# A three-way windowed attention kernel: the wide projection moved ahead of the third unit of scores

## The chip, the cores and the metric

The kernel runs on one core of one Trainium2 chip. The metric is the device time of one launch in microseconds (us). Engines go by short names: PE (TensorE, matmuls), ACT (ScalarE), DVE (VectorE), POOL (GpSimd), SP (SyncE, which here only issues transposing DMAs).

## What is computed

The input is 128 x 256 x 192. A tokenizer stage first turns each of the 128 sequences of 256 rows into 127 pooled rows of 192 (a gated softmax over windows of four). Then come an attention block and a feed-forward block, each on a layer norm of its input and each added back. The reference of the attention block, cut to what matters:

```python
qkv = (x @ w_qkv.T).reshape(B, N, 3, H, hd)        # H = 8 heads, hd = 24, thirds of 8
q3, q4, q5 = thirds(q); k3, k4, k5 = thirds(k); v3, v4, v5 = thirds(v)
x3 = attn(q4, cat(k3, k4), cat(v3, v4))            # softmax(q k^T * scale) v
x4 = attn(q5, cat(k3, k5), cat(v3, v5))
x5 = attn(q5, cat(k4, k5), cat(v4, v5))
out = cat(x3, x4, x5) @ w_proj.T + b_proj
h = h + out
```

## The kernel before

One block is one sequence (127 rows of 192), and there are NB = 128 blocks. The function `attend` runs the whole attention stage as a software pipeline written out by hand: every engine has a `body(i, r)`, called for i = -4 to 130 (r is i modulo 4), and in body i the engines work on different blocks. Engines meet only through semaphores, each engine takes its instructions in the order in which the body writes them, and all transposing DMAs go through SP in the order of its body.

In one body PE does, in this order:

- `products(i, r, 0)` to `products(i, r, 3)`, four *units* of two heads. A unit has six matmuls of *scores* (L583) into three PSUM tiles, `p_s1`, `p_s5` and `p_s0`, for block i, and four matmuls of *maxima* (L587) into `p_maxa` (two matmuls of 384 columns) and `p_maxb`. The maxima are plain q k^T products that serve only to find each row's largest value for a later block: block i+1 in units 0 and 1, block i+2 in units 2 and 3.
- between the units: `outputs` (L653, probabilities times values, into `p_o`; eight matmuls after unit 0, eight after unit 1, eight after unit 3), `qkv(i)` (the *wide projection* of block i+3 into `p_z`, five matmuls of 512 columns, L620 to L626, after unit 2), `outputs_t` (three transposes of `ot`, L664, after the wide projection) and `proj` (the output projection of block i-2, also into `p_z`, after unit 3).

ACT does three exponentials a unit, each of 128x512: of `p_s1` (L696), `p_s5` (L700) and `p_s0` (L703). After unit 1 it copies `p_o` to `ot` (L712), and after the exponentials of unit 2 it copies the wide projection out of `p_z`, the q and k part to `raw` (L721), the v part to `vn` (L722). There is one `p_z`, so `proj` waits for the copy to `vn`.

DVE reduces `p_maxa` (L746) and `p_maxb` (L750) in each unit, takes the layer norm's statistics (L757, `bn_stats`), writes the maxima into the operand `qk` (L766, L767), normalizes (L773, L776) and adds `proj` to the residual (L783). Each of the tiles `p_s1`, `p_s5`, `p_s0`, `p_maxa` and `p_maxb` exists once, so the matmuls of one unit wait for the readers of the unit before: `p_s0` for L703, `p_maxa` for L746, `p_maxb` for L750.

POOL splits `raw` into high and low halves in `qk` (`halves`, L801 to L812). SP then transposes: `kt` and `qt` (needed by the maxima of unit 2 in the next body), `qm` (needed by the scores), `xt` (needed by the wide projection) and `yt` (needed by `proj`).

Of the kernel before, what the change touches and what calls it, by code (L numbers as in the profile page):

```python
# [12 lines left out]
C = 192  # L13
# [437 lines left out]
def attend(nc, t, NB):  # L451

    with ExitStack() as ctx:
# [3 lines left out]
        U = 4  # L457
        NQ, NK = 3 * HEADS, 3 * HEADS
        K0 = NQ * 32
# [62 lines left out]
        def _(sp):  # L522
# [6 lines left out]
            def body(i, r):  # L529
# [5 lines left out]
                if within(i + 2, NB):  # L535
                    ready(pool_k, seen(i + 3))
                    if within(i - 2, NB):
                        ready(pe_s0[3], seen(i - 1))
                    sp.dma_start_transpose(kt[:, (r + 2) % U].rearrange("p k g n -> p (k g) n"), qk[:, r % 2, K0:K0 + 768]).then_inc(dma_k, 16)
                    ready(pool_q, seen(i + 3))  # L540
                    if within(i, NB):
                        ready(pe_ma[1], seen(2 * (i + 1)))
                        ready(pe_mb[1], seen(i + 1))
                    sp.dma_start_transpose(qt[:, r % 2].rearrange("p k g n -> p (k g) n"), qk[:, r % 2, 0:512]).then_inc(dma_q, 16)
# [24 lines left out]
        def _(pe):  # L569
# [3 lines left out]
            def products(i, r, u):  # L573
# [15 lines left out]

                if has_s:  # L590
# [4 lines left out]
                if has_m:  # L595
                    if u == 2:
                        pe.wait_ge(dma_k, seen(16 * (bm + 1)))
                        pe.wait_ge(dma_q, seen(16 * (bm + 1)))
                    pe.wait_ge(dve_ma[u - 1], seen(i + 2 if u < 3 else i + 3))
                    maximum(p_ma[:, 0:3, :], c, 1, slice(0, 3)).then_inc(pe_ma[u], 1)  # L600
                    maximum(p_ma[:, 4:7, :], d, 1, slice(0, 3)).then_inc(pe_ma[u], 1)
                if has_s:
                    score(p_s[1][:, 2:4, :], b, 1, slice(0, 3, 2)).then_inc(pe_s1[u], 1)
                if has_s:
                    pe.wait_ge(act_e5[u - 1] if u else act_e5[3], seen(i + 1 if u else i))
                    score(p_s5[:, 0:2, :], fifth, 2, slice(1, 3), 0)
                    score(p_s5[:, 2:4, :], fifth, 2, slice(1, 3), 1).then_inc(pe_half[u], 1)
# [20 lines left out]
            def qkv(i):  # L628
                if within(i + 3, NB):
                    pe.wait_ge(dma_x, seen(16 * (i + 4)))  # L630
                    pe.wait_ge(*z_reader(i, 0))
                    rows(p_z[:, :], xt, "wqkv").then_inc(pe_qkv, 1)
# [34 lines left out]
            def body(i, r):  # L667
# [10 lines left out]
                outputs(i - 1, before, 1, 2)  # L678

                products(i, r, 2)  # L680
                qkv(i)
# [9 lines left out]
        def _(act):  # L691
# [14 lines left out]
            def body(i, r):  # L706
# [7 lines left out]
                exponentials(i, r, 2)  # L714
# [9 lines left out]

                exponentials(i, r, 3)
# [484 lines left out]
```

## Time and profile before

| | |
|---|---|
| three runs | 1880.60, 1873.08, 1877.03 us; median 1877.03 us |
| the profiled execution | 1871.97 us, its span 1870.2 us |
| busy in the span | PE 94%, DVE 80%, ACT 77%, POOL 67%, PE's weight loads 54% |
| mean granted TensorE clock | 0.981 of full |
| attention stage | its first wide projection starts at 343.0 us, its last output projection at 1418.6 us |

A matmul's end is modelled, so a high busy share of PE is no proof that PE never waits: what a wait costs has to be read off the start times. Views that follow later are read like this. A row of a timeline is start (us), duration (us), engine, line, operation, output<-input tiles, shapes and count; square brackets hold the idle time of the engine just before it and who ended it, and rows between two "..." are left out. A row of the windows view holds the window's bounds, its length, busy us (and instructions) of PE, PE's weight loads, DVE, ACT and POOL, the granted TensorE clock as a share of full, the share of DMA time and GB/s. A grouped row holds line, engine, operation, tiles and count, then busy us and mean ns of one, then idle us of the engine just before them and who ended it. A DMA row ends with the median us from issue to landing.

The tokenizer comes before the attention stage and the feed-forward block after it; the change touches neither.

### The profile page before, as it was taken

The page shows a single profiled execution, that of the slowest core. Times are in us where ns is not written, and L with a number is a line of the kernel's source. Part 1 is how long each engine was busy: PE and PEld are TensorE (multiplying, and loading weights), DVE is VectorE, ACT ScalarE, POOL GpSimd, SP SyncE. Part 2 cuts the span into 40 slices and gives each one's busy share as a digit, 9 for nine tenths or more (in the row PEclk, how much of TensorE's full clock was granted, in tenths as well). Part 3 has the DMA queues.
Part 4 walks back from the last instruction along what each step waited for, and adds up shares of the span by engine and source line. Part 5 has one row for each costly group of instructions (what it writes and reads, how often), then busy time and mean ns, then how long its engine had stood idle before and what let it go on. Part 6 is the DMA issues. An engine that isn't in the chain of part 4 may idle for free. (4 is left out here: it accounts for less than half of the span.)

```text
span 1870.2 us, 56704 instructions
## 1 busy us (share of the span) xinstructions
PE 1749.2 (94%) x19008; PEld 1016.4 (54%) x19008; DVE 1498.9 (80%) x3546; ACT 1444.0 (77%) x2983; POOL 1251.8 (67%) x2306
## 2 busy tenths in 40 slices
PE   5999999589999999999999999999994999999999
PEld 3677777144444444444444444444442777777776
DVE  6877778589999999999999999999984555555554
ACT  4666666288888888888888888888884777777775
POOL 5777776477777777777777777777753565656661
PEclk9999999599999999999999999999997999999999
DMA  7344442154444444444444444444441333333332
GB/s 192 95 111 111 111 111 67 39 83 89 86 90 89 89 87 90 89 89 87 89 90 88 89 89 90 88 89 89 89 76 28 71 69 69 70 67 70 67 74 54
DMA packets 503935, 159.49 MB, mean 85 GB/s; under 512 B 452176, under 2 KB 503120, under 8 KB 503888
## 3 DMA queue, kind: packets, MB, share of 16 engines
q1 hardware_dynamic: 503888, 158.90, 40.1%
q8 instruction: 26, 0.43, 0.1%
q14 instruction: 21, 0.17, 0.0%
HBM read 37.26 MB, written 12.48 MB: 27 GB/s over the span
## 5 line engine op out<-in xcount | busy, mean ns | idle before, releaser
L746 DVE TENSOR_REDUCE tops<-p_maxa 128x6 f32<-128x762 f32 x512 | 483.7, 945 | 50.5 <-PE p_maxa L587 38.9
L653 PE MATMUL p_o<-probs,vn 127*32 127x256 f32 x6144 | 410.7, 385 | 0.4 <-DVE att L776 0.4
L696 ACT ACTIVATE probs<-p_s 128x512 f32<-128x512 f32 x512 | 306.3, 598 | 126.6 <-PE p_s L583 126.3
L583 PE MATMUL p_s<-qm,kt 32*128 32x256 f16 x3072 | 369.9, 272 | 3.3
L750 DVE TENSOR_REDUCE tops<-p_maxb 128x4 f32<-128x508 f32 x512 | 346.6, 677 | 0.0
L703 ACT ACTIVATE probs<-p_s 128x512 f32<-128x512 f32 x512 | 310.9, 607 | 0.0
L700 ACT ACTIVATE probs<-p_s 128x512 f32<-128x512 f32 x512 | 304.0, 594 | 0.0
L1055 DVE TENSOR_TENSOR gel_lo<-gel,gel_hi 128x512 f16<-128x512 f32 x192 | 151.2, 788 | 168.1 <-ACT gel_hi L1027 168.1
L583 PEld LDWEIGHTS p_s<-qm,kt 32*128 32x128 f16 x3072 | 149.3, 92 | 229.3 <-issue 126.4
L801 POOL TENSOR_TENSOR qk<-raw,one 128x384 f16<-128x384 f32 x128 | 105.7, 826 | 228.2 <-ACT raw L721 228.2
L653 PEld LDWEIGHTS p_o<-probs,vn 127*32 127x32 f32 x6144 | 160.5, 109 | 140.6 <-issue 74.4
L1019 ACT ACTIVATE gel<-f_w,b 128x512 f32<-128x512 f32 x192 | 131.9, 687 | 117.4 <-PE f_w L968 117.4
L587 PE MATMUL p_maxa<-kt,qt 24*128 24x384 f16 x1024 | 173.4, 333 | 37.3 <-issue 18.8
L587 PE MATMUL p_maxb<-kt,qt 24*128 24x256 f16 x1024 | 196.5, 272 | 0.2
L979 PE MATMUL f_y<-w_hi,gel_hi 128*128 128x192 f16 x768 | 188.8, 246 | 0.2 <-DVE gel_lo L1055 0.2
L981 PE MATMUL f_y<-w_hi,gel_lo 128*128 128x192 f16 x768 | 188.9, 246 | 0.0
L980 PE MATMUL f_y<-w_lo,gel_hi 128*128 128x192 f16 x768 | 188.8, 246 | 0.0
L1125 POOL TENSOR_TENSOR f_hx<-f_hn,f_one 128x192 f16<-128x192 f32 x120 | 85.5, 712 | 153.7 <-ACT f_hn L1006 151.0
L208 ACT ACTIVATE tanhs<-pa 128x384 f32<-128x384 f32 x128 | 62.7, 490 | 99.2 <-PE pa L154 99.2
L1027 ACT ACTIVATE gel_hi<-gel 128x512 f16<-128x512 f32 x192 | 120.9, 630 | 7.0
L396 POOL TENSOR_TENSOR diag<-ident,weight 128x256 f32<-128x256 f32 x128 | 79.2, 620 | 54.1 <-DVE weight L296 44.9
L183 PE MATMUL ph<-zs,band 128*128 128x192 f32 x512 | 105.4, 330 | 3.1 <-DVE band L317 2.2
(212 smaller groups left out, 4509.9 us busy)
## 6 DMA issues: line engine op xcount, KB each, us to landing
xt_a<-in_xt SPq DMA_DIRECT2D x32, 512.0 KB, 4.4
xt_b<-in_xt SPq DMA_DIRECT2D x64, 256.0 KB, 5.1
out<-out_sb SPq DMA_DIRECT2D x32, 336.0 KB, 2.6
xt<-hx SPq DMA_TRANSPOSE x128, 2.4
kt<-qk SPq DMA_TRANSPOSE x128, 2.8
qt<-qk SPq DMA_TRANSPOSE x128, 2.4
qm<-qk SPq DMA_TRANSPOSE x128, 2.7
yt<-ay SPq DMA_TRANSPOSE x128, 2.3
```

Source lines behind the costliest of these rows:

```text
L583: return nc.tensor.matmul(o, kt[full(j), r, kind, half, :], qm[full(j), r % 2, versions, half, :], start=True, stop=True, skip_group_check ...
L587: return nc.tensor.matmul(o, qt[short(j), rq, kind, half, :], kt[short(j), rk, cols, half, :], start=True, stop=True, skip_group_check=True)
L653: last = nc.tensor.matmul(p_o[32 * j:32 * j + 32, blocks, :], vn[0:NP, r, src:src + 32], probs[0:NP, r % 2, QUAD * g + j, kind * 256:(kind ...
L696: nc.scalar.activation(probs[:, r % 2, h + 1, 0:512], p_s[1][:, :, :].rearrange("p x n -> p (x n)"), ACT.Exp, scale=SCALE).then_inc(act_e1 ...
L700: nc.scalar.activation(probs[:, r % 2, fifth:HEADS:QUAD, 512:768], p_s5[:, :, :].rearrange("p (h x) n -> p h (x n)", h=2), ACT.Exp, scale= ...
L703: nc.scalar.activation(probs[:, r % 2, h, 0:512], p_s[0][:, :, :].rearrange("p x n -> p (x n)"), ACT.Exp, scale=SCALE).then_inc(act_e0[u], 1)
L746: nc.vector.tensor_reduce(top[:, q, 6 * pair:6 * pair + 6].rearrange("p (e k) -> p e k", e=2), p_ma[:, :, :].rearrange("p (e k) n -> p e k ...
L750: nc.vector.tensor_reduce(top[:, q, 24 + 4 * fourth:28 + 4 * fourth], p_mb[:, :, 0:NP], AX.X, ALU.max, negate=True)\
L979: nc.tensor.matmul(o, ghi[:, c % 3, n], t.w2_hi[:, c, :], start=False, stop=False)
L980: nc.tensor.matmul(o, ghi[:, c % 3, n], t.w2_lo[:, c, :], start=False, stop=False)
L981: last = nc.tensor.matmul(o, glo[:, c % 3, n], t.w2_hi[:, c, :], start=False, stop=(c == HCH - 1))
L1055: nc.vector.tensor_tensor(glo[:, c % 3, :], gel[:, c % 2, :], ghi[:, c % 3, :], ALU.subtract).then_inc(dve_lo[c], 1)
```

## The change

On PE, `qkv(i)` is split into `qkv_begin` (three matmuls) and `qkv_end` (two), both called one after the other ahead of `products(i, r, 2)`, where `qkv(i)` stood behind it. In unit 2 alone, the matmuls of `p_s1` and `p_s5` are issued ahead of those of `p_maxa` (and of the wait for the transposed `kt` and `qt`). On ACT, the copies to `raw` and `vn` stand ahead of the exponentials of unit 2. On DVE, `bn_stats` stands behind unit 1 and its two writes of `qk`, where it stood behind unit 0. On SP, the waits that guard the slots of `kt` and `qt` are all taken ahead of the wait for POOL's k, one wait (for the maxima of unit 2 of the body before) being new. No operation is added or removed.

```diff
--- before.py
+++ after.py
@@ -533,14 +533,16 @@
                         ready(pe_qkv, seen(i + 3))
                     sp.dma_start_transpose(xt[:, :, :], hx[:, (r + 1) % 2, :]).then_inc(dma_x, 16)
                 if within(i + 2, NB):
-                    ready(pool_k, seen(i + 3))
-                    if within(i - 2, NB):
-                        ready(pe_s0[3], seen(i - 1))
-                    sp.dma_start_transpose(kt[:, (r + 2) % U].rearrange("p k g n -> p (k g) n"), qk[:, r % 2, K0:K0 + 768]).then_inc(dma_k, 16)
-                    ready(pool_q, seen(i + 3))
+                    if within(i + 1, NB):
+                        ready(pe_ma[2], seen(2 * (i + 2)))
                     if within(i, NB):
                         ready(pe_ma[1], seen(2 * (i + 1)))
                         ready(pe_mb[1], seen(i + 1))
+                    if within(i - 2, NB):
+                        ready(pe_s0[3], seen(i - 1))
+                    ready(pool_k, seen(i + 3))
+                    sp.dma_start_transpose(kt[:, (r + 2) % U].rearrange("p k g n -> p (k g) n"), qk[:, r % 2, K0:K0 + 768]).then_inc(dma_k, 16)
+                    ready(pool_q, seen(i + 3))
                     sp.dma_start_transpose(qt[:, r % 2].rearrange("p k g n -> p (k g) n"), qk[:, r % 2, 0:512]).then_inc(dma_q, 16)
                 if within(i - 2, NB):
                     ready(pool_y, seen(i - 1))
@@ -587,24 +589,35 @@
                     return nc.tensor.matmul(o, qt[short(j), rq, kind, half, :], kt[short(j), rk, cols, half, :],
                                             start=True, stop=True, skip_group_check=True)
 
+                def large(do):
+
+                    if do:
+                        if u == 2:
+                            pe.wait_ge(dma_k, seen(16 * (bm + 1)))
+                            pe.wait_ge(dma_q, seen(16 * (bm + 1)))
+                        pe.wait_ge(dve_ma[u - 1], seen(i + 2 if u < 3 else i + 3))
+                        maximum(p_ma[:, 0:3, :], c, 1, slice(0, 3)).then_inc(pe_ma[u], 1)
+                        maximum(p_ma[:, 4:7, :], d, 1, slice(0, 3)).then_inc(pe_ma[u], 1)
+
+                def odd(do):
+
+                    if do:
+                        score(p_s[1][:, 2:4, :], b, 1, slice(0, 3, 2)).then_inc(pe_s1[u], 1)
+                        pe.wait_ge(act_e5[u - 1] if u else act_e5[3], seen(i + 1 if u else i))
+                        score(p_s5[:, 0:2, :], fifth, 2, slice(1, 3), 0)
+                        score(p_s5[:, 2:4, :], fifth, 2, slice(1, 3), 1).then_inc(pe_half[u], 1)
+
                 if has_s:
                     if u == 0:
                         pe.wait_ge(dma_qm, seen(16 * (i + 1)))
                     pe.wait_ge(act_e1[u - 1] if u else act_e1[3], seen(i + 1 if u else i))
                     score(p_s[1][:, 0:2, :], b, 0, slice(0, 2))
-                if has_m:
-                    if u == 2:
-                        pe.wait_ge(dma_k, seen(16 * (bm + 1)))
-                        pe.wait_ge(dma_q, seen(16 * (bm + 1)))
-                    pe.wait_ge(dve_ma[u - 1], seen(i + 2 if u < 3 else i + 3))
-                    maximum(p_ma[:, 0:3, :], c, 1, slice(0, 3)).then_inc(pe_ma[u], 1)
-                    maximum(p_ma[:, 4:7, :], d, 1, slice(0, 3)).then_inc(pe_ma[u], 1)
-                if has_s:
-                    score(p_s[1][:, 2:4, :], b, 1, slice(0, 3, 2)).then_inc(pe_s1[u], 1)
-                if has_s:
-                    pe.wait_ge(act_e5[u - 1] if u else act_e5[3], seen(i + 1 if u else i))
-                    score(p_s5[:, 0:2, :], fifth, 2, slice(1, 3), 0)
-                    score(p_s5[:, 2:4, :], fifth, 2, slice(1, 3), 1).then_inc(pe_half[u], 1)
+                if u == 2:
+                    odd(has_s)
+                    large(has_m)
+                else:
+                    large(has_m)
+                    odd(has_s)
                 if has_s:
                     pe.wait_ge(act_e0[u - 1] if u else act_e0[3], seen(i + 1 if u else i))
                     score(p_s[0][:, 0:2, :], a, 0, slice(0, 2))
@@ -625,11 +638,19 @@
                     nc.tensor.matmul(o, ones16[:, :], bias[:, :], start=False, stop=False)
                 return nc.tensor.matmul(o, x[:, 2, :], t.third[name][:, :], start=False, stop=True)
 
-            def qkv(i):
+            def qkv_begin(i):
+                wa, wl, wb, wbl = t.split["wqkv"]
                 if within(i + 3, NB):
                     pe.wait_ge(dma_x, seen(16 * (i + 4)))
                     pe.wait_ge(*z_reader(i, 0))
-                    rows(p_z[:, :], xt, "wqkv").then_inc(pe_qkv, 1)
+                    nc.tensor.matmul(p_z[:, :], xt[:, 0, :], wa[:, :], start=True, stop=False)
+                    nc.tensor.matmul(p_z[:, :], xt[:, 0, :], wl[:, :], start=False, stop=False)
+                    nc.tensor.matmul(p_z[:, :], xt[:, 1, :], wb[:, :], start=False, stop=False)
+
+            def qkv_end(i):
+                if within(i + 3, NB):
+                    nc.tensor.matmul(p_z[:, :], xt[:, 1, :], t.split["wqkv"][3][:, :], start=False, stop=False)
+                    nc.tensor.matmul(p_z[:, :], xt[:, 2, :], t.third["wqkv"][:, :], start=False, stop=True).then_inc(pe_qkv, 1)
 
             def proj(i):
                 if within(i - 2, NB):
@@ -676,9 +697,10 @@
                 products(i, r, 1)
                 outputs(i - 1, before, 1, 1)
                 outputs(i - 1, before, 1, 2)
+                qkv_begin(i)
+                qkv_end(i)
 
                 products(i, r, 2)
-                qkv(i)
                 outputs_t(i)
 
                 products(i, r, 3)
@@ -711,7 +733,6 @@
                     act.wait_ge(pe_pv, seen(i))
                     nc.scalar.activation(ot[:, :, :], p_o[:, 0:3, :], ACT.Copy).then_inc(act_ot, 1)
 
-                exponentials(i, r, 2)
                 if within(i + 3, NB):
                     act.wait_ge(pe_qkv, seen(i + 4))
                     if isinstance(i, int) and i == -3:
@@ -722,6 +743,7 @@
                     nc.scalar.activation(vn[:, (r + 3) % U, :].rearrange("p (s d) -> p s d", d=32)[:, :, 0:G8],
                                          p_z[:, 320:512].rearrange("p (s d) -> p s d", d=G8), ACT.Copy).then_inc(act_v, 1)
 
+                exponentials(i, r, 2)
                 exponentials(i, r, 3)
             loop(act, body)
 
@@ -752,9 +774,6 @@
 
             def body(i, r):
                 maxima(i, r, 0)
-                if within(i - 3, NB):
-                    dve.wait_ge(dve_h, seen(i - 2))
-                    nc.vector.bn_stats(t.stats[:, bass.ds((i - 3) * 6, 6)], t.h[:, bass.ds((i - 3) * C, C)])
 
                 maxima(i, r, 1)
                 if within(i + 1, NB):
@@ -765,6 +784,10 @@
                     low = slots((r + 1) % 2, 0, NQ)[:, :, 24].rearrange("p (x h) -> p x h", x=3)
                     nc.vector.tensor_tensor(low[:, 0].rearrange("p (g j) -> p g j", g=2), of4[:, 0], of4[:, 1], ALU.min)
                     nc.vector.tensor_tensor(low[:, 1:3], of5[:, 0:2], of5[:, 2:3].broadcast_to([128, 2, HEADS]), ALU.min).then_inc(dve_min, 1)
+
+                if within(i - 3, NB):
+                    dve.wait_ge(dve_h, seen(i - 2))
+                    nc.vector.bn_stats(t.stats[:, bass.ds((i - 3) * 6, 6)], t.h[:, bass.ds((i - 3) * C, C)])
 
                 maxima(i, r, 2)
                 if within(i - 1, NB):
```

PE in the first body that has all the parts but the output projection, before, from the last `outputs` behind unit 1 onwards (names in brackets are the semaphores that a matmul waits for; `act_e11` is ACT's exponential of `p_s1` in unit 1):

```order
L653 MATMUL p_o<-probs,vn 32x256 x4
L583 MATMUL p_s1<-qm,kt 128x256 [waits act_e11]
L587 MATMUL p_maxa<-kt,qt 128x384 [waits dve_ma1,dma_q,dma_k]
L587 MATMUL p_maxa<-kt,qt 128x384
L583 MATMUL p_s1<-qm,kt 128x256
L583 MATMUL p_s5<-qm,kt 128x256 [waits act_e51]
L583 MATMUL p_s5<-qm,kt 128x256
L583 MATMUL p_s0<-qm,kt 128x256 [waits act_e01]
L583 MATMUL p_s0<-qm,kt 128x256
L587 MATMUL p_maxb<-kt,qt 128x256 [waits dve_mb1]
L587 MATMUL p_maxb<-kt,qt 128x256
L620 MATMUL p_z<-wqkv_ahi,xt 128x512 [waits act_v,dma_x]
```

The same stretch of PE in the changed program:

```order
L674 MATMUL p_o<-probs,vn 32x256 x4
L646 MATMUL p_z<-wqkv_ahi,xt 128x512 [waits act_v,dma_x]
L647 MATMUL p_z<-wqkv_alo,xt 128x512
L648 MATMUL p_z<-wqkv_bhi,xt 128x512
L652 MATMUL p_z<-wqkv_blo,xt 128x512
L653 MATMUL p_z<-wqkv_chi,xt 128x512
L585 MATMUL p_s1<-qm,kt 128x256 [waits act_e11]
L585 MATMUL p_s1<-qm,kt 128x256
L585 MATMUL p_s5<-qm,kt 128x256 [waits act_e51]
L585 MATMUL p_s5<-qm,kt 128x256
L589 MATMUL p_maxa<-kt,qt 128x384 [waits dve_ma1,dma_q,dma_k]
L589 MATMUL p_maxa<-kt,qt 128x384
```

The five matmuls of the wide projection moved from behind the unit to ahead of it, and the two of `p_maxa`, with the wait for `dma_q` and `dma_k`, from second place in the unit to fifth.

ACT before, from the last exponential of unit 1 to the second of unit 3 (`pe_s12` is PE's `p_s1` of unit 2):

```order
L703 ACTIVATE probs<-p_s 128x512 [waits pe_s01]
L712 ACTIVATE ot<-p_o 128x384 [waits pe_pv]
L696 ACTIVATE probs<-p_s 128x512 [waits pe_s12]
L700 ACTIVATE probs<-p_s 128x2x256 [waits pe_half2]
L703 ACTIVATE probs<-p_s 128x512 [waits pe_s02]
L721 ACTIVATE raw<-p_z 128x320 [waits pool_q,pe_qkv]
L722 ACTIVATE vn<-p_z 128x24x8
L696 ACTIVATE probs<-p_s 128x512 [waits pe_s13]
L700 ACTIVATE probs<-p_s 128x2x256 [waits pe_half3]
```

ACT in the changed program:

```order
L725 ACTIVATE probs<-p_s 128x512 [waits pe_s01]
L734 ACTIVATE ot<-p_o 128x384 [waits pe_pv]
L742 ACTIVATE raw<-p_z 128x320 [waits pool_q,pe_qkv]
L743 ACTIVATE vn<-p_z 128x24x8
L718 ACTIVATE probs<-p_s 128x512 [waits pe_s12]
L722 ACTIVATE probs<-p_s 128x2x256 [waits pe_half2]
L725 ACTIVATE probs<-p_s 128x512 [waits pe_s02]
L718 ACTIVATE probs<-p_s 128x512 [waits pe_s13]
L722 ACTIVATE probs<-p_s 128x2x256 [waits pe_half3]
```

The two copies out of `p_z`, and with them the wait for `pe_qkv`, moved from behind the three exponentials of unit 2 to ahead of them.

## Rows read from the trace of the kernel before

**Rows 1.** The windows view: engines' busy time at the start and mid attention.

```profile
330.00:380.00 50.00, 27.48 (x175) 9.84 (x174) 30.50 (x57) 16.53 (x35) 24.80 (x52) 0.62 0.22 45
500.00:1300.00 800.00, 768.12 (x10060) 369.05 (x10052) 752.74 (x1380) 704.25 (x1477) 591.41 (x1185) 1.00 0.44 89
```

**Rows 2.** The grouped view, 500 to 1300 us: the wider maxima.

```profile
L746 DVE TENSOR_REDUCE tops<-p_maxa 128x6 f32<-128x762 f32 x395 | 373.1, 944 | 21.6 <-PE p_maxa L587 12.5
```

**Rows 3.** Timeline of PE, one attention body and the next one's first row.

```profile
801.26 0.28 PE L583 MATMUL p_s<-qm,kt 32*128 32x256 f16 x1
...
803.34 0.28 PE L587 MATMUL p_maxb<-kt,qt 24*128 24x256 f16 x1
...
803.65 1.07 PE L653 MATMUL p_o<-probs,vn 127*32 127x256 f32 x16
804.66 0.28 PE L583 MATMUL p_s<-qm,kt 32*128 32x256 f16 x1
805.04 0.34 PE L587 MATMUL p_maxa<-kt,qt 24*128 24x384 f16 x2
...
805.52 0.39 PE L620 MATMUL p_z<-wqkv_ahi,xt 128*128 128x512 f16 x1
...
806.40 0.38 PE L626 MATMUL p_z<-wqkv_chi,xt 128*128 128x512 f16 x1
...
807.33 0.27 PE L587 MATMUL p_maxb<-kt,qt 24*128 24x256 f16 x1
807.73 0.24 PE L620 MATMUL p_z<-wproj_ahi,yt 128*128 128x192 f16 x1
...
808.32 1.07 PE L653 MATMUL p_o<-probs,vn 127*32 127x256 f32 x16
809.32 0.28 PE L583 MATMUL p_s<-qm,kt 32*128 32x256 f16 x1
```

**Rows 4.** Timeline of ACT over the same body.

```profile
801.70 0.60 ACT L696 ACTIVATE probs<-p_s 128x512 f32<-128x512 f32 x1 [0.70 <-PE p_s L583]
...
802.67 0.61 ACT L703 ACTIVATE probs<-p_s 128x512 f32<-128x512 f32 x1
...
805.46 0.60 ACT L696 ACTIVATE probs<-p_s 128x512 f32<-128x512 f32 x1 [0.18 <-PE p_s L583]
...
806.91 0.46 ACT L721 ACTIVATE raw<-p_z 128x320 f32<-128x320 f32 x1
807.22 0.37 ACT L722 ACTIVATE vn<-p_z 128x192 f32<-128x192 f32 x1
807.48 0.60 ACT L696 ACTIVATE probs<-p_s 128x512 f32<-128x512 f32 x1
...
808.45 0.61 ACT L703 ACTIVATE probs<-p_s 128x512 f32<-128x512 f32 x1
809.76 0.60 ACT L696 ACTIVATE probs<-p_s 128x512 f32<-128x512 f32 x1 [0.70 <-PE p_s L583]
```

**Rows 5.** Timeline of the SP queue: the transposition of q.

```profile
802.54 1.19 SPq L544 DMA_TRANSPOSE qt<-qk  x1
```

**Rows 6.** The DMA view, 500 to 1300 us: median us to landing.

```profile
qt<-qk SPq DMA_TRANSPOSE x99, 2.4
```

**Rows 7.** Timeline of DVE over the same body.

```profile
805.43 0.95 DVE L746 TENSOR_REDUCE tops<-p_maxa 128x6 f32<-128x762 f32 x1
...
807.14 0.31 DVE L773 RECIPROCAL att_inv<-p_o 128x24 f32<-128x24 f32 x1 [0.17 <-PE p_o L664]
...
809.73 0.95 DVE L746 TENSOR_REDUCE tops<-p_maxa 128x6 f32<-128x762 f32 x1 [0.17 <-PE p_maxa L587]
810.60 0.68 DVE L750 TENSOR_REDUCE tops<-p_maxb 128x4 f32<-128x508 f32 x1
```

**Rows 8.** Timeline of PE at the start of attention: two wide projections.

```profile
352.82 0.61 PE L620 MATMUL p_z<-wqkv_ahi,xt 128*128 128x512 f16 x1
...
361.93 0.61 PE L620 MATMUL p_z<-wqkv_ahi,xt 128*128 128x512 f16 x1
```

## The prediction

> **What bounds the kernel now.** I read the windows view first. Between 500 and 1300 us, in the middle of attention, PE is busy 768 us of 800 and DVE 753, at a granted clock of 1.00, which is the 2.4 GHz level [rows 1]. Neither share says what sets the pace: PE's rows overlap and their ends are modelled, and DVE has waits ahead of some of its rows. The grouped view gives the period: 395 of the wider reductions, four a body, in 800 us, so 98.75 bodies at 8.10 us each [rows 2]. Then I laid the timelines of PE and ACT over one body and followed back what each late start waited for. The chain closes on itself:
>
> - ACT starts the first exponential of unit 0 at 801.70 and ends the third at 802.67 + 0.61 = 803.28 [rows 4]: 1.58 us.
> - PE may then overwrite `p_s0`: the end of its unit 1 starts at 803.34 (0.06), the eight `outputs` behind it at 803.65 (0.31), unit 2 at 804.66 (1.01) [rows 3].
> - In unit 2 the first score goes at 804.66, but the maxima behind it only at 805.04 [rows 3]. Their transposed q was issued at 802.54 and takes 2.4 to land, which is 804.94 [rows 5, 6]. The second score of `p_s1` is queued behind them, so ACT's first exponential of unit 2 starts at 805.46, 0.80 after 804.66, and ACT stood idle 0.18 for it [rows 4].
> - ACT does three exponentials and two copies until 807.22 + 0.37 = 807.59: 2.13 us [rows 4]. The output projection waits for the copy of v, since both use `p_z`: PE could go on soon after 807.33, but it starts at 807.73 (0.14 behind the copy) [rows 3].
> - Output projection to `outputs` at 808.32 (0.59), to the next unit 0 at 809.32 (1.00), to ACT's next first exponential at 809.76 (0.44), for which ACT idled 0.70 [rows 3, 4].
>
> The sum is 1.58 + 0.06 + 0.31 + 1.01 + 0.80 + 2.13 + 0.14 + 0.59 + 1.00 + 0.44 = 8.06, the distance from 801.70 to 809.76. So the period is a ring of ACT and PE waiting for each other. The wide projection, 805.52 to 806.78 on PE [rows 3], is not in this ring: it runs while ACT does the exponentials of unit 2.
>
> **The change on this ring.** *Up to the end of `outputs` behind unit 1 nothing changes*: 1.58 + 0.06 + 0.31 + 1.01 = 2.96.
>
> *The wide projection comes next on PE, and ACT has nothing to do until it is over.* The copies stand ahead of the exponentials of unit 2, so ACT's next work waits for the last of five matmuls. From the first start to the last end is 806.40 + 0.38 - 805.52 = 1.26, and 0.05 for ACT to begin (as 0.06 the other way): 1.31 where 0.80 stood. The late transposition goes out of the ring with this: a gain of the 0.38 between 804.66 and 805.04, already counted, since 1.31 replaces the whole 0.80.
>
> *The copies, then the exponentials.* 807.48 - 806.91 = 0.57 for the two copies, then 808.45 + 0.61 - 807.48 = 1.58 for three exponentials [rows 4]: 2.15 where 2.13 stood. Unit 2's first scores are on PE right behind the projection, five times 0.22 behind its start, so they are ready before ACT comes out of the copies.
>
> *Unit 3 to the output projection.* `p_s0` of unit 3 may be written once the third exponential of unit 2 has ended. Before, that was hidden behind the copies and the projection started 0.14 after them. Now the last exponential is itself the last link: 0.06 to PE's last scores, and 0.31 from there to whatever follows the unit, as behind unit 1. 0.37 where 0.14 stood. Then 0.59 + 1.00 + 0.44 as before.
>
> Sum of the ring after: 2.96 + 1.31 + 0.57 + 1.58 + 0.37 + 0.59 + 1.00 + 0.44 = 8.82, against 8.06: **0.76 us more a body** (0.51 + 0.02 + 0.23).
>
> *The reordered unit 2 and DVE.* There is a second ring, of DVE and PE, since `p_maxb` of unit 1 waits for DVE's reduction in unit 0, and the matmuls behind it wait with it. DVE from unit 2 to the next unit 0 takes 809.73 - 805.43 = 4.30, of which 0.17 + 0.17 are waits [rows 7]: 3.96. Then to the end of the narrower reduction 810.60 + 0.68 - 809.73 = 1.55, then 0.06 + 0.31 + 1.01 on PE as above. Before, unit 2's maxima could follow at once, with 0.34 + 0.05 until DVE starts: 7.28, far inside 8.10. Now the wide projection (five starts 0.22 apart, 1.10) and three matmuls of 256 columns (half of that spacing each, 0.33) are ahead of them: 8.71. That is 0.11 below the other ring, so it does not decide, but it holds the period near 8.7 even if ACT's ring is shorter than I think. DVE, which has 0.34 of waits in this stretch now, will stand idle about 1 us a body ahead of unit 2's reduction.
>
> *The statistics.* `bn_stats` goes from one place between DVE's reductions to another in the same body. It costs nothing either way as long as DVE waits ahead of unit 2: it now fills part of that wait. Without that cover it would still be the same row.
>
> *SP's waits.* The guards now taken ahead of the wait for k concern readers a whole body back, so they have passed. The new one (maxima of unit 2 of the body before) too. Behind them on SP stand `yt`, `qm` and the next `xt`, none moved. The q transposition is issued with fewer waits between it and k's, and its source is earlier: the copy to `raw` starts 2.96 + 1.31 = 4.27 after unit 0's first exponential where it was 806.91 - 801.70 = 5.21. Its reader comes 1.10 + 0.33 later in the next body, which itself is 0.76 later: a slack of some 3 us in place of a wait of 0.38. If that cover were gone, only maxima would wait, since the scores of `p_s1` and `p_s5` now stand ahead.
>
> **How many bodies.** The wide projection and the scores share bodies 0 to 124. In the first three the pipeline still fills: two wide projections start 9.11 apart there, 352.82 to 361.93, at matmuls of 0.61 instead of 0.39 and a mean clock of 0.62 [rows 1, 8]. There the projection stood behind a unit that waits for its transposed q and k, and now it stands ahead and can run while they fly. A filling body gains between nothing and the projection's own time at the 1.2 GHz level, 5 x 0.43 = 2.15 (twice the spacing of rows 3). I take 4 us for three bodies, bounds 0 and 6. So 122 x 0.76 = 93, less 4: **+89 us** on the profiled execution's own 1872, which is 1961. The median of the runs shown is 1877, 0.3% above it, and would give 1966; I say 1963.
>
> **A rule against a row.** In rows 3 the wide projection's starts are 0.22 apart (0.88 for four). The Trainium skill ("TensorE: Matmul & The Clock Gate", Back-to-back issue gap) gives a sustained spacing of about 131 ns for 512 columns in a stream of weight loads and matmuls. By that figure five of them would take 0.66, an estimate, and the sum would fall to about +35 us. This case's trace does not bear it out for this stream, and the rival below has its price from rows.
>
> **Rivals.**
>
> 1. *The ring of ACT and PE as above*, 1963: 0.70.
> 2. *Only DVE's ring holds.* If the 0.23 behind unit 3 is hidden after all (PE's small matmuls queued early enough), ACT's ring is 8.59 and DVE's 8.71 decides: +0.65 x 122 - 4 = 75, so 1948. 0.13. For it: DVE's busy share. Against: unit 1 shows exactly that 0.31.
> 3. *The projection costs about half*, because part of it overlaps the tail of `outputs` (rows of 1.07 whose followers start after 1.01): two of its five spacings off both rings is 0.44, leaving 0.32 x 122 - 4 = 35, so 1911. 0.05. Against: every follower of `outputs` in rows 3 starts 1.00 or 1.01 behind it, and the projection needs the whole array.
> 4. *Faster: the late transposition is what costs, and the projection hides.* Then the 0.38 ahead of 805.04 goes and nothing comes back: 122 x -0.38 - 4 = -50, so 1825. It decides if PE reaches the projection 0.51 or more ahead of the moment at which ACT runs out of work. For it: the wait is there in every body. Against: ACT was idle only 0.18 ahead of that exponential, so ACT runs dry almost at once behind unit 1 and cannot cover 1.31. 0.05. An outcome within 0.5% would need half of this hiding: 0.03.
> 5. *The clock falls.* PE's waits grow from a few per cent to some 12% of the body. The granted clock was 1.00 throughout and 0.62 in the filling phase, where PE was busy 27.5 us of 50 [rows 1]. If bodies ran at 1.2 GHz, the projection alone would cost 1.1 us more: 122 x 1.1 = 134 on top, 2097 or more. 0.04. PE would still be busy well over 80% of each body, far from those 27.5 in 50.
>
> **The numbers.** The likeliest is 1963. Its own bounds: 8.7 to 8.95 a body and 0 to 6 us at the start, 1945 to 1981. To hold 8 in 10 with the neighbours and a waiting time on each side that no row prices, 1930 to 1990. Half a per cent, some 9 us, is about what a measurement of this kernel can tell from no change. Faster by more: 0.05 and a little for mechanisms that I have not seen, 0.06; the same 0.03; slower 0.91.
>
> **What the profile after would show.** Period 8.8 (395 reductions in some 870 us). In PE's timeline, `outputs` behind unit 1, five wide matmuls 0.22 apart, then unit 2 with no gap. On ACT an idle time of about 0.7 ahead of the copy to `raw`, released by PE's wide projection, and about 0.9 ahead of unit 0. On DVE about 1 us idle ahead of unit 2's wider reduction, none ahead of the reciprocal. The output projection starting 0.37 after the third exponential of unit 2. Transposed q landed long before its reader. I would be wrong if PE reached the wide projection early, with ACT still busy when it ends, or if a period below 8.5 showed.

## The result, and the profile after

The changed kernel takes 1952.76 us (median of 4 runs, 1948.28 to 1953.76), the kernel before beside it 1875.56. The ratio is 1.0403, with a 95% interval of 1.0375 to 1.0432: 4.0% slower, +77 us where the prediction's sum had +89 and its 1963 lies 87 above that 1875.56.

The page of the changed kernel's profiled execution:

```profile
span 1946.5 us, 56830 instructions
...
PE 1819.4 (93%) x19008; PEld 1016.4 (52%) x19008; DVE 1469.5 (75%) x3546; ACT 1447.3 (74%) x2983; POOL 1254.8 (64%) x2306
```

The span grew by 76.3 us, from 1870.2 to 1946.5. PE's busy time grew by 70 us (from 1749.2) with the same number of matmuls at a mean clock of 0.983 (0.981 before). Its rows overlap and their ends are modelled, so this is no count of work: it is the timeline that shows the loss.

The grouped view, 500 to 1300 us, answers to [rows 2]:

```profile
L768 DVE TENSOR_REDUCE tops<-p_maxa 128x6 f32<-128x762 f32 x364 | 345.2, 948 | 119.7 <-PE p_maxa L589 108.0
...
L742 ACT ACTIVATE raw<-p_z 128x320 f32<-128x320 f32 x90 | 39.4, 438 | 61.4 <-PE p_z L653 61.4
```

364 wider reductions in 800 us are 91 bodies of 8.79 us, where 395 rows made 98.75 bodies of 8.10. Such a count is rough, since a body can be cut at either end of the window. Taken from one wide projection's start to the next, the bodies go in fours: 8.81, 8.80, 8.81 and 8.88 here, 8.13, 8.15, 8.16 and 8.06 before. The means over the 116 settled steps are 8.83 and 8.13. The second row is the copy to `raw`: 61.4 us of idle time in front of its 90, 0.68 each, ended by PE. The view of waits for the same stretch names three idle times that belong to the change (us in total, times, longest us):

```profile
DVE tops L768 <- PE p_maxa L589: 108.0, 91, 1.2
ACT probs L718 <- PE p_s L585: 86.5, 91, 1.0
...
ACT raw L742 <- PE p_z L653: 61.4, 90, 0.7
```

DVE stands idle 1.2 a body ahead of unit 2's wider reduction, ACT 0.95 ahead of unit 0's first exponential (0.70 before, [rows 4]). Now the timeline of PE over one body, to be laid beside [rows 3]:

```profile
868.09 0.39 PE L646 MATMUL p_z<-wqkv_ahi,xt 128*128 128x512 f16 x1
...
868.97 0.38 PE L653 MATMUL p_z<-wqkv_chi,xt 128*128 128x512 f16 x1
869.28 0.28 PE L585 MATMUL p_s<-qm,kt 32*128 32x256 f16 x2
...
871.58 0.28 PE L589 MATMUL p_maxb<-kt,qt 24*128 24x256 f16 x1
...
871.90 0.26 PE L633 MATMUL p_z<-wproj_ahi,yt 128*128 128x192 f16 x1
...
872.50 1.07 PE L674 MATMUL p_o<-probs,vn 127*32 127x256 f32 x16
873.50 0.28 PE L585 MATMUL p_s<-qm,kt 32*128 32x256 f16 x1
```

Unit 1's outputs are followed at 868.09 by the wide projection, and unit 2's scores start at 869.28, 1.19 later. There is no gap ahead of unit 2's maxima any more. ACT over the same body, beside [rows 4]:

```profile
865.13 0.60 ACT L718 ACTIVATE probs<-p_s 128x512 f32<-128x512 f32 x1 [0.95 <-PE p_s L585]
...
866.10 0.61 ACT L725 ACTIVATE probs<-p_s 128x512 f32<-128x512 f32 x1
...
869.38 0.44 ACT L742 ACTIVATE raw<-p_z 128x320 f32<-128x320 f32 x1 [0.66 <-PE p_z L653]
...
869.93 0.61 ACT L718 ACTIVATE probs<-p_s 128x512 f32<-128x512 f32 x1
...
870.88 0.63 ACT L725 ACTIVATE probs<-p_s 128x512 f32<-128x512 f32 x1
...
873.94 0.60 ACT L718 ACTIVATE probs<-p_s 128x512 f32<-128x512 f32 x1 [0.95 <-PE p_s L585]
```

From 865.13 to 873.94 the period is 8.81. ACT's idle 0.66 ahead of 869.38 is the rest of the time in which PE does the projection: ACT has only the copy to `ot` to do meanwhile (868.23, 0.49 us). The third exponential of unit 2 ends at 870.88 + 0.63 = 871.51, PE's last matmuls of unit 3 start at 871.58 and the output projection at 871.90, 0.39 behind it. DVE, beside [rows 7]:

```profile
869.91 0.95 DVE L768 TENSOR_REDUCE tops<-p_maxa 128x6 f32<-128x762 f32 x1 [1.21 <-PE p_maxa L589]
...
871.37 0.30 DVE L796 RECIPROCAL att_inv<-p_o 128x24 f32<-128x24 f32 x1
...
873.91 0.95 DVE L768 TENSOR_REDUCE tops<-p_maxa 128x6 f32<-128x762 f32 x1
```

The reduction of unit 2 waits 1.21, the reciprocal no longer waits for PE.

### The profile page after: what moved, and what is told of

The parts are those of the page before. It is cut to its first block and busy times, and to the rows that moved or that the text cites. A ratio compares the mean times of both kernels' runs of the same rounds, so it can differ in the third digit from the quotient of the medians.

```text
span 1946.5 us, 56830 instructions
## 1 busy us (share of the span) xinstructions
PE 1819.4 (93%) x19008; PEld 1016.4 (52%) x19008; DVE 1469.5 (75%) x3546; ACT 1447.3 (74%) x2983; POOL 1254.8 (64%) x2306
## 5 line engine op out<-in xcount | busy, mean ns | idle before, releaser
L585 PE MATMUL p_s<-qm,kt 32*128 32x256 f16 x3072 | 402.6, 273 | 52.1 <-ACT probs L718 35.9
L718 ACT ACTIVATE probs<-p_s 128x512 f32<-128x512 f32 x512 | 313.5, 612 | 121.7 <-PE p_s L585 121.6
L725 ACT ACTIVATE probs<-p_s 128x512 f32<-128x512 f32 x512 | 321.7, 628 | 0.0
L722 ACT ACTIVATE probs<-p_s 128x512 f32<-128x512 f32 x512 | 314.7, 615 | 0.0
L589 PE MATMUL p_maxa<-kt,qt 24*128 24x384 f16 x1024 | 199.2, 333 | 8.5 <-DVE tops L768 2.8
L742 ACT ACTIVATE raw<-p_z 128x320 f32<-128x320 f32 x128 | 56.1, 438 | 109.0 <-PE p_z L653 109.0
```

The source lines that it names most:

```text
L585: return nc.tensor.matmul(o, kt[full(j), r, kind, half, :], qm[full(j), r % 2, versions, half, :], start=True, stop=True, skip_group_check ...
L589: return nc.tensor.matmul(o, qt[short(j), rq, kind, half, :], kt[short(j), rk, cols, half, :], start=True, stop=True, skip_group_check=True)
L718: nc.scalar.activation(probs[:, r % 2, h + 1, 0:512], p_s[1][:, :, :].rearrange("p x n -> p (x n)"), ACT.Exp, scale=SCALE).then_inc(act_e1 ...
L722: nc.scalar.activation(probs[:, r % 2, fifth:HEADS:QUAD, 512:768], p_s5[:, :, :].rearrange("p (h x) n -> p h (x n)", h=2), ACT.Exp, scale= ...
L725: nc.scalar.activation(probs[:, r % 2, h, 0:512], p_s[0][:, :, :].rearrange("p x n -> p (x n)"), ACT.Exp, scale=SCALE).then_inc(act_e0[u], 1)
```

## The experiments

Ten kernels were timed. "The changed kernel" is the one of the diff above. Ratios are to the kernel before, run beside them.

**1. The rest of the change without its two moves.** The projection goes back behind unit 2 on PE and the copies back behind unit 2's exponentials on ACT; the reordered unit 2, SP's guards and the place of the statistics stay as changed.

```diff
-                qkv_begin(i)
-                qkv_end(i)
                 products(i, r, 2)
+                qkv_begin(i)
+                qkv_end(i)
...
+                exponentials(i, r, 2)
                 if within(i + 3, NB):
                     act.wait_ge(pe_qkv, seen(i + 4))
...
-                exponentials(i, r, 2)
                 exponentials(i, r, 3)
```

> The changed kernel with the wide projection put back behind unit 2 on PE and its copies back behind unit 2's exponentials on ACT; the reordered unit 2, SP's guards and the statistics stay as changed. Theory (the loss is the projection, put into the ring of ACT and PE): the loss goes, and what is left of the change shortens the old ring. ACT's 0.80 from PE's unit 2 to its exponential falls to about 0.51 (the copy of p_o then ends last), and the second ring, raw to POOL to the transposed q to unit 2's maxima to the projection to raw, falls from 8.05 by the 0.27 by which q now follows k sooner on SP: 7.8 a body, about -37 us on the kernel before, 1838. Rival (the reordered unit 2 with its later maxima starves DVE, or the moved statistics cost): it stays well above the kernel before, 1900 or more.

Measured: 1849.54 us, ratio 0.9872 (0.9853 to 0.9890). So the two moves together cost 1.0403 - 0.9872 = 5.3% (99 us) and the rest of the change gives 1.3% (23 us). The rival falls. The gain is smaller than the 37 us expected, since the period is 7.92 and not 7.8, and SP's queue shows why. Its rows for one body (the three are `xt`, `kt`, `qt`):

```profile
805.17 1.19 SPq L534 DMA_TRANSPOSE xt<-hx  x1
807.00 1.21 SPq L544 DMA_TRANSPOSE kt<-qk  x1
808.33 1.19 SPq L546 DMA_TRANSPOSE qt<-qk  x1
```

POOL's low half of k, for which `kt` waits, and PE's maxima of unit 2 in this body and in the next:

```profile
805.80 0.55 POOL L827 TENSOR_TENSOR qk<-raw,qk 128x192 f16<-128x192 f32 x1
```

```profile
802.61 0.34 PE L589 MATMUL p_maxa<-kt,qt 24*128 24x384 f16 x2
...
810.85 0.34 PE L589 MATMUL p_maxa<-kt,qt 24*128 24x384 f16 x2 [0.28 <-issue]
```

POOL ended at 806.35 and SP was through with `xt` at 806.36, but `kt` went at 807.00: the guards, taken one by one between them, took the 0.64. `qt` followed at 808.33, and PE waited 0.28 for it ahead of 810.85. That is one body of four here: from one projection's start to the next it takes 8.23 to 8.26, the three others 7.70, 7.86 and 7.96.

**2. The projection ahead on PE alone**, the copies behind unit 2's exponentials again.

```diff
+                exponentials(i, r, 2)
                 if within(i + 3, NB):
                     act.wait_ge(pe_qkv, seen(i + 4))
...
-                exponentials(i, r, 2)
                 exponentials(i, r, 3)
```

> The changed kernel with only ACT's copies put back behind the exponentials of unit 2; the projection stays ahead on PE. Theory: the ring has the projection in it either way, 2.96 + 1.19 + 0.38 + 2.13 + 0.14 + 0.60 + 1.00 + 0.44 = 8.84 a body against 8.81, so 1955 or the same as the changed kernel. Rival (the copies ahead of the exponentials are what costs): 0.25 to 0.6 a body less, 1880 to 1922.

Measured: 1956.45 us, ratio 1.0446 (1.0427 to 1.0465), 0.4% above the changed kernel. Only PE's order differs between experiment 1 and this one, and it is worth 1.0446 - 0.9872 = 5.7%. So the move on PE explains the loss by itself, and ACT's order then hardly matters. Copies ahead of the exponentials are, with the projection early, slightly the better order.

**3. The copies ahead on ACT alone**, the projection behind unit 2 on PE again.

```diff
-                qkv_begin(i)
-                qkv_end(i)
                 products(i, r, 2)
+                qkv_begin(i)
+                qkv_end(i)
```

> The changed kernel with only the projection put back behind unit 2 on PE; the copies stay ahead of the exponentials on ACT. Theory (ring of ACT and PE): unit 2's 0.86 on PE and then the projection's 1.31 both stand between the outputs and ACT: 8.81 + 0.86 = 9.67 a body, about +106 us on the changed kernel, 2058. Rival (the ring of DVE and PE decides): that ring loses the projection here, 1.10, and would let the kernel fall to the old 8.1 a body, 1876 or less.

Measured: 2133.21 us, ratio 1.1385 (1.1363 to 1.1406), more than either theory. The rival (DVE's ring decides) falls, since that ring lost the projection here and the kernel became slower still, also in bodies at the full clock. The size has two parts. PE's timeline, a wait of the body before (991.76), then one projection and the next:

```profile
991.76 0.28 PE L585 MATMUL p_s<-qm,kt 32*128 32x256 f16 x1 [0.91 <-ACT probs L718]
...
1000.06 0.39 PE L646 MATMUL p_z<-wqkv_ahi,xt 128*128 128x512 f16 x1
...
1002.55 0.28 PE L585 MATMUL p_s<-qm,kt 32*128 32x256 f16 x1 [0.91 <-ACT probs L718]
...
1008.86 0.28 PE L585 MATMUL p_s<-qm,kt 32*128 32x256 f16 x2
...
1009.36 0.39 PE L646 MATMUL p_z<-wqkv_ahi,xt 128*128 128x512 f16 x1
```

From 1000.06 to 1009.36 this body takes 9.30, not 9.67: unit 2 takes 0.50 on PE (1008.86 to 1009.36) and not 0.86, as I had carried over the 0.38 for the late transposition. But 97 projections lie between 508.1 and 1490.4, so the mean body is 10.23. The windows view of the body before it, which took 10.80 (989.26 to 1000.06), shows what others lose (columns as in [rows 1]); the last row lies in the body of 9.30:

```profile
990.00:992.00 2.00, 1.09 (x10) 0.52 (x8) 1.50 (x4) 1.45 (x4) 0.85 (x2) 1.00 0.50 98
992.00:994.00 2.00, 1.80 (x20) 0.85 (x20) 1.64 (x2) 2.00 (x5) 1.84 (x4) 0.83 0.33 67
994.00:996.00 2.00, 2.00 (x22) 0.65 (x24) 0.36 (x1) 0.15 (x1) 1.84 (x6) 0.50 0.75 146
996.00:998.00 2.00, 2.00 (x32) 0.78 (x24) 1.54 (x2) 1.57 (x3) 1.48 (x3) 0.81 0.24 49
998.00:1000.00 2.00, 2.00 (x34) 0.85 (x30) 1.90 (x5) 1.90 (x4) 0.00 (x0) 1.00 0.00 0
...
1002.00:1004.00 2.00, 1.24 (x12) 0.47 (x13) 1.31 (x2) 2.00 (x6) 1.84 (x4) 1.00 0.42 83
```

The granted clock fell to 0.50, the 1.2 GHz level, after a stretch in which PE was busy 1.09 us of 2. It came back by 998. The mean clock between 500 and 1500 us is 0.90; over the whole execution it is 0.921, and 0.979 to 0.983 in the profiled executions of all other kernels here. Of 24 bodies in a row from 713 us on, the ten at a mean clock of 1.00 take 9.29 to 9.38 and the fourteen at 0.84 take 10.80 to 10.94, so the 0.93 a body between 9.30 and 10.23 is this. PE's wait does not tell them apart: it is 0.91 in the body that lost the clock and 0.91 in the next, where PE was busy 1.24 us of 2 and the clock stayed at 1.00. What takes the clock down in some bodies and not in others stays open.

**4. The projection cut short in the changed kernel.** Two of its five matmuls, those with the low halves of the weights, are left out.

```diff
-                    nc.tensor.matmul(p_z[:, :], xt[:, 0, :], wl[:, :], start=False, stop=False)
...
-                    nc.tensor.matmul(p_z[:, :], xt[:, 1, :], t.split["wqkv"][3][:, :], start=False, stop=False)
```

> The changed kernel with two of the five matmuls of the wide projection left out (the products with the low halves of the weights, so q, k and v are less exact); nothing else changes. Theory: the projection lies whole on the path, so 2 x 0.22 = 0.44 a body go, 0.44 x 123 = 54 us, 1899. Rival (it is hidden at least in part, and something else holds the period): 1930 to 1952.

Measured: 1897.18 us, ratio 1.0133 (1.0112 to 1.0154). The changed kernel's 1.0403 less this is 0.027 of the time before, 51 us, for 54 expected. From start to start of the projections a body takes 8.37 and every fourth 8.44 or 8.45, where the changed kernel has 8.81 and 8.88: 0.44 less. Two matmuls at their full spacing of 0.22 are 0.44, so their whole time comes back. That is the mark of work on the path.

**5. The statistics behind unit 3 in the changed kernel.**

```diff
-                if within(i - 3, NB):
-                    dve.wait_ge(dve_h, seen(i - 2))
-                    nc.vector.bn_stats(...)
...
                     nc.vector.tensor_tensor(t.h[...], p_z[:, 0:C], t.h[...], ALU.add).then_inc(dve_h, 1)
+                if within(i - 3, NB):
+                    dve.wait_ge(dve_h, seen(i - 2))
+                    nc.vector.bn_stats(...)
```

> The changed kernel with the statistics (0.26 us of DVE from start to start) moved from behind unit 1 to behind unit 3, that is from DVE's idle time ahead of unit 2 into the stretch of DVE's ring. It weighs the second ring. Theory (ring of ACT and PE at 8.81, ring of DVE and PE just below, 8.60 by the rows of the changed kernel): 8.60 + 0.26 = 8.86 takes over, +0.05 x 123 = 6 us on the changed kernel, 1958. Rival (DVE's ring is the one that holds the period): the whole 0.26, +32, 1985. If DVE's ring were far below, nothing: 1952.

Measured: 1949.78 us, ratio 1.0416 (1.0399 to 1.0432), the changed kernel within the intervals. The grouped view, 500 to 1300 us:

```profile
L768 DVE TENSOR_REDUCE tops<-p_maxa 128x6 f32<-128x762 f32 x364 | 343.2, 943 | 129.0 <-PE p_maxa L589 129.0
```

The same 364 reductions, with 129.0 us idle ahead of them where the changed kernel has 119.7, and the same period, 8.80 from start to start (8.81 there). The third case, 1952, came true and not the theory's 1958. DVE's ring is not the one that decides, and with 0.26 more it still fits under 8.80: it is 8.80 - 0.26 = 8.54 or less in the changed kernel, and I had worked out 8.60.

**6. SP's part alone, on the kernel before.**

```diff
                 if within(i + 2, NB):
-                    ready(pool_k, seen(i + 3))
+                    if within(i + 1, NB):
+                        ready(pe_ma[2], seen(2 * (i + 2)))
+                    if within(i, NB):
+                        ready(pe_ma[1], seen(2 * (i + 1)))
+                        ready(pe_mb[1], seen(i + 1))
                     if within(i - 2, NB):
                         ready(pe_s0[3], seen(i - 1))
+                    ready(pool_k, seen(i + 3))
                     sp.dma_start_transpose(kt...)
                     ready(pool_q, seen(i + 3))
-                    if within(i, NB):
-                        ready(pe_ma[1], seen(2 * (i + 1)))
-                        ready(pe_mb[1], seen(i + 1))
                     sp.dma_start_transpose(qt...)
```

> The kernel before with SP's part of the change alone (all guards of kt and qt ahead of the wait for k). Theory: q's transposition follows k's 0.27 sooner, PE's wait of 0.38 in unit 2 shrinks to 0.11, ACT can use 0.18 of that, and the ring over POOL and SP falls from 8.05 to 7.8: 7.9 a body, about -22 us, 1852. Rival (guards on SP are free wherever they stand, the 0.27 is lost elsewhere on SP's queue): no change, 1873.

Measured: 1855.23 us, ratio 0.9905 (0.9889 to 0.9921), -18 us for 22 expected. Taking three satisfied waits at another place on SP, with a fourth added there, is worth 1%. The kernel before issues q's transposition at 802.54 [rows 5], 1.54 behind k's:

```profile
801.00 1.21 SPq L539 DMA_TRANSPOSE kt<-qk  x1
```

Here the two are 1.33 apart (800.12 and 801.45).

**7. The reordered unit 2 alone, on the kernel before.**

```diff
+                if u == 2:
+                    odd(has_s)
+                    large(has_m)
+                else:
+                    large(has_m)
+                    odd(has_s)
```

> The kernel before with the reordered unit 2 alone (scores of p_s1 and p_s5 ahead of the maxima and of the wait for the transposed q). Theory: ACT's ring gets 0.29 shorter, but the ring raw, POOL, SP, transposed q, unit 2's maxima, projection, raw stays at 8.05, so nothing is gained: 1868 to 1876. Rival (only ACT's ring matters): 7.8 a body, 1838.

Measured: 1865.04 us, ratio 0.9957 (0.9944 to 0.9971), -8 us. The rival (-35) falls. ACT's ring alone does not set the old period: with it shortened by 0.29 the body went only from 8.10 to 8.02 (399 reductions in 800 us). It is more than the nothing that was expected, but the ring that the theory named is there. The copy to `raw`, the transpositions of k and q, the next unit 2's maxima, the projection and the next copy:

```profile
803.08 0.44 ACT L741 ACTIVATE raw<-p_z 128x320 f32<-128x320 f32 x1
...
805.21 1.21 SPq L539 DMA_TRANSPOSE kt<-qk  x1
806.81 1.19 SPq L544 DMA_TRANSPOSE qt<-qk  x1
...
809.32 0.34 PE L587 MATMUL p_maxa<-kt,qt 24*128 24x384 f16 x2
...
809.81 0.39 PE L644 MATMUL p_z<-wqkv_ahi,xt 128*128 128x512 f16 x1
...
811.10 0.44 ACT L741 ACTIVATE raw<-p_z 128x320 f32<-128x320 f32 x1
```

2.13 from the copy to k's transposition (POOL's k ends at 805.05), 1.60 to q's, 2.51 to the maxima (q takes 2.4 to land), 0.49 to the projection and 1.29 to the next copy are 8.02. ACT was through with its exponentials at 810.96 and took the copy at 811.10, behind the projection.

**8. Experiment 1 without the guards**, where the wait for the projection that SP takes ahead of `xt` already covers them.

```diff
-                    if within(i + 1, NB):
+                    if not within(i + 3, NB):
                         ready(pe_ma[2], seen(2 * (i + 2)))
-                    if within(i, NB):
-                        ready(pe_ma[1], seen(2 * (i + 1)))
-                        ready(pe_mb[1], seen(i + 1))
-                    if within(i - 2, NB):
                         ready(pe_s0[3], seen(i - 1))
```

> The first experiment's kernel (projection and copies put back, rest of the change kept) with SP's four guards of kt and qt left out wherever the wait for the projection ahead of xt already covers them. In that experiment one body of four still waits 0.28 for the transposed q, and there SP issued k 0.65 behind POOL's end, the guards between. Theory: that wait goes, and the period falls from 7.92 to ACT's ring at about 7.77: -18 us on the first experiment, 1831. Rival (the guards cost nothing, DVE or the copies hold 7.92): 1849.

Measured: 1832.85 us, ratio 0.9779 (0.9763 to 0.9796). It beats both kernels. The grouped view, 500 to 1300 us:

```profile
L764 DVE TENSOR_REDUCE tops<-p_maxa 128x6 f32<-128x762 f32 x411 | 387.8, 943 | 5.3
```

411 reductions make 7.79 a body, and DVE is idle only 5.3 us ahead of them. From here on DVE's own work is close to the period.

**9. Experiment 1 with the projection inside unit 2**, behind its scores and ahead of its maxima.

```diff
                 if u == 2:
                     odd(has_s)
-                    large(has_m)
...
                     score(p_s[0][:, 2:4, :], a, 1, slice(0, 3, 2)).then_inc(pe_s0[u], 1)
+                if u == 2:
+                    qkv_begin(i)
+                    qkv_end(i)
+                    large(has_m)
```

> The first experiment's kernel (copies behind unit 2's exponentials) with the wide projection between unit 2's six scores and its maxima, so that ACT has its scores at once and only the maxima stand behind the projection. It isolates the ring of DVE and PE. Theory: ACT's ring stays at 7.8, but DVE's ring gets the projection, 3.87 + 1.54 + 0.06 + 0.31 + 1.01 + 0.64 (scores) + 1.20 (projection) + 0.40 = 9.03, or 8.94 with the 0.09 by which the run with the moved statistics measured that ring shorter: +1.02 x 122 = 124 us on the first experiment, 1973. Rival (only the ring of ACT and PE matters): as the first experiment, 1849.

Measured: 1975.82 us, ratio 1.0546 (1.0522 to 1.0571), for 1973 expected. From start to start a body takes 8.99 to 9.05. So ACT is not the only one that must not be kept waiting. PE's timeline, and DVE's rows of unit 2:

```profile
802.93 0.61 PE L585 MATMUL p_s<-qm,kt 32*128 32x256 f16 x6
803.47 0.39 PE L649 MATMUL p_z<-wqkv_ahi,xt 128*128 128x512 f16 x1
...
804.65 0.34 PE L589 MATMUL p_maxa<-kt,qt 24*128 24x384 f16 x2
...
806.07 0.34 PE L589 MATMUL p_maxa<-kt,qt 24*128 24x384 f16 x2 [0.17 <-DVE tops L769]
...
806.66 0.39 PE L589 MATMUL p_maxb<-kt,qt 24*128 24x256 f16 x2
...
811.98 0.28 PE L585 MATMUL p_s<-qm,kt 32*128 32x256 f16 x2
```

```profile
805.06 0.95 DVE L769 TENSOR_REDUCE tops<-p_maxa 128x6 f32<-128x762 f32 x1 [1.46 <-PE p_maxa L589]
805.92 0.68 DVE L773 TENSOR_REDUCE tops<-p_maxb 128x4 f32<-128x508 f32 x1
```

The maxima start at 804.65 and DVE at 805.06 after 1.46 of idle time. The wider reduction ends at 806.01, and only then can PE write unit 3's wider maxima (806.07), with unit 3's scores queued behind them, so ACT is late too. The narrower one ends at 805.92 + 0.68 = 806.60, and it is the one that the path goes through: PE writes unit 3's `p_maxb` at 806.66, and the output projection follows. From unit 2 to unit 2 it is 811.98 - 802.93 = 9.05. The size came out as expected, but the path is DVE's two reductions of unit 2 and then the ring of ACT and PE again. DVE's own ring is just below: its reductions of unit 0 end at 810.54, ACT's third exponential at 810.59, and PE goes on at 810.66. That the expected sum, made for DVE's ring alone, met the time is in part luck.

**10. Experiment 8 with the statistics back behind unit 0.**

```diff
                 maxima(i, r, 0)
+                if within(i - 3, NB):
+                    dve.wait_ge(dve_h, seen(i - 2))
+                    nc.vector.bn_stats(...)
```

> The fastest kernel so far (projection and copies put back, guards left out) with the statistics back behind unit 0, where the kernel before has them. Theory: DVE is idle only some 15 us in 800 there, so its own work sets the period, and it costs the same wherever the row stands: no change, 1833. Rival (behind unit 0 it delays unit 1's reduction and with it q's maxima for SP): 5 to 15 us more.

Measured: 1830.53 us, ratio 0.9768 (0.9748 to 0.9788), the same as experiment 8. The statistics' place is worth nothing that can be measured, here as in experiment 5.

## Why the prediction was right, point by point

**The ring of ACT and PE: right.** The period worked out was 8.82 and 8.81 was measured. Its new links, by this execution's rows: outputs to the copy 869.38 - 868.09 = 1.29 (1.31 said), copies 0.55 (0.57), three exponentials 1.58 (1.58), last exponential to output projection 0.39 (0.37). Experiments 2 and 3 put the projection and the copies on that path one by one, and experiment 4 got all of the projection's removed time back.

**The size of the loss: 77 where 89 was said, and the mis-sized term is the period before.** I subtracted the ring of one body, 8.06, and that body is the shortest of each four (8.13, 8.15, 8.16, 8.06). By the means, 8.83 and 8.13, the loss is 0.70 a body and not 0.76. Experiments 6 and 7 show what I had missed in reading that body. Each part shortens ACT's way to its exponentials, and they give 1.0% and 0.4%, which add up to the 1.3% of experiment 1, still with a wait in one body of four; without the guards it is 2.2%. The kernel before hung on two rings of nearly one length: ACT's, and the one from the copy to `raw` over POOL and SP to the transposed q and back to the projection, which experiment 7's rows show closed at 8.02. I had named the late transposition only as a link of ACT's ring.

**The filling of the pipeline: the number came out, its working did not.** The first output projection started 5.2 us earlier (386.5, 391.7 before), of which 1.2 came from ahead of the attention stage (first wide projection 341.8 and 343.0). 4.0 is left for the 4 said. But [rows 8] do not lie in bodies 0 to 2, as I had it: they are steps ahead of the first scores, and the three steps there take 22.76 where they took 28.19. Nor do all of 122 bodies lose the full amount. Of the 127 steps from one wide projection to the next, the first nine gain 4.5 us (76.15 for 80.61), the 116 settled ones lose 81.1, and the last two gain 0.9 (17.62 for 18.51). That is 75.8, and the span grew by 76.3.

**DVE's ring: right that it is second, 8.71 said and at most 8.54 measured.** Its idle time was 1.21, not 1. So rival 2, in which it alone held the period, had more distance to go than I gave it, and experiment 5 shows no trace of it. Experiment 9 shows that DVE's reductions still enter the path when the maxima are kept back longer.

**SP's waits: priced at nothing, which fits the changed kernel, where the transposed q has slack, but not the kernel before.** There the same edit gives 1%. I had its mechanism in the text (q follows k sooner) but priced it only behind a ring that hid it.

**The statistics: right**, by experiments 5 and 10.

**The other rivals.** The half-hidden projection (rival 3) is not borne out: the five starts stand 0.22 apart (868.09 to 868.97 for four), and removing two of them gave 0.44 a body. The Trainium skill ("TensorE: Matmul & The Clock Gate", Back-to-back issue gap) gives a sustained spacing of about 131 ns for 512 columns. This trace does not agree: it shows 0.22 us. The faster rival is told apart by experiments 1 and 2: the wait for the transposed q is worth something only where the projection stays out of the way. The falling clock (rival 5) did not come in the changed kernel, where the mean stayed at 0.983, but it came in experiment 3, whose bodies at full clock are only 0.49 longer. So the rival's distance from the 27.5 us of 50 was no safe argument.

## What to carry to other kernels

When engines wait for each other in a ring, lay one body of the timeline out link by link, from an engine's start to its next start, and see which work is not in it: moving that work to where it looks natural can put it in, at its full length, though no engine got more work. Then look for a second ring of nearly the same length before pricing a gain, and take the period from many bodies rather than from the one on the page. A queue that issues DMAs also pays for each wait that it takes, satisfied or not, so guards belong where the queue has time, or nowhere if an earlier wait covers them (experiments 6 and 8, 18 and 17 us).

## What the runs showed of the hardware that I had not expected

- The granted clock of experiment 3 fell to 0.50 in some bodies, and its mean in mid attention was 0.90, with PE waiting 0.91 us at a time for ACT and busy 889 us of 1000. The changed kernel, with waits of 0.27 at the same place, kept 1.00, but so did the bodies of experiment 3 that took 9.3 with the same 0.91. The fall cost some 0.93 a body in the mean, more than the 0.49 by which the body grew at full clock.
- Satisfied waits on SP are not free. Between k's and q's transposition stand three waits in the kernel before, and q is issued 1.54 after k (801.00 and 802.54). In experiment 1 one wait stands there, and the two are 1.33 apart (807.00 and 808.33). By these numbers a wait costs some 0.1, an estimate, and the four guards ahead of k with the wait for POOL took 0.64.
